# Banded attention in a fourteen-stage decoder kernel: the division is moved from the weights to the results, and the last chunk's order is rewritten

## The reference, cut to what matters

```python
_OFFSETS = list(range(41)) + [128, 96, 384]
idx = jnp.arange(T)[:, None] - deltas[None, :]
valid = idx >= 0
k_mod = k_g * (1.0 + scale_embed)
scores = jnp.einsum('bhtd,bhtjd->bhtj', q, k_mod) * scale
scores = scores + pos_bias.T[None, :, None, :]
scores = jnp.where(valid[None, None], scores, jnp.finfo(scores.dtype).min)
attn = jax.nn.softmax(scores, axis=-1)
out = jnp.einsum('bhtj,bhtjd->bhtd', attn, v_g)
out = out * if_gain[None, :, None, None]
out = out.transpose(0, 2, 1, 3).reshape(B, T, C)
return out @ w_out
```

## Time and profile before

| | |
|---|---|
| median of 3 runs | 3556.07 us (3554.3 to 3569.99) |
| profiled execution, its time | 3591.05 us |
| its span, mean granted TensorE clock | 3589.0 us, 0.94 |
| busy: TensorE matmuls, VectorE, ScalarE, GpSimd | 3165.8, 1804.1, 1185.1, 927.7 us |
| the stage: first product to last statistics | about 27 to 348 us |
| of it, chunks 1 to 3 and ending | 70 to 301 us, 301 to 348 us |

### The profile page before, as it was taken

The page is one execution under the profiler, slowest core; times in us unless marked ns, Lnnn a source line. Parts: engine busy times, 40 slices in busy tenths (PEclk is TensorE's granted clock), DMA queues, the critical chain, the costliest instruction groups (busy, mean ns, idle before and its releaser), DMA issues. The chain is left out here.

```text
span 3589.0 us, 74982 instructions
## 1 busy us (share of the span) xinstructions
PE 3165.8 (88%) x30324; PEld 2191.8 (61%) x30324; DVE 1804.1 (50%) x4518; ACT 1185.1 (33%) x2326; POOL 927.7 (26%) x771
## 2 busy tenths in 40 slices
PE   8886999999987878877777999779998899999989
PEld 3333555555666764655644555569997786566656
DVE  8887544543233463442386666543333663355543
ACT  1222323323223323221234556422222462144433
POOL 1000442442000000423426878611111210104001
PEclk9998999999989988988888999979999899999989
DMA  4223000000132020533601111068887200021100
GB/s 150 57 65 93 20 9 17 9 9 8 43 55 24 4 47 6 163 111 103 200 20 47 30 30 30 7 253 326 329 331 259 90 14 13 19 74 52 52 14 19
DMA packets 173982, 287.22 MB, mean 80 GB/s; under 512 B 79184, under 2 KB 144261, under 8 KB 164338
## 3 DMA queue, kind: packets, MB, share of 16 engines
q1 hardware_dynamic: 166194, 262.48, 23.5%
q0 software_dynamic: 7488, 20.46, 1.7%
HBM read 244.49 MB, written 28.48 MB: 76 GB/s over the span
## 5 line engine op out<-in xcount | busy, mean ns | idle before, releaser
L2646 PE MATMUL ps<-L_ffn_xsT,arena 128*128 128x128 f32 x2584 | 311.8, 280 | 20.2 <-DVE L_ffn_xsT L2445 16.1
L2646 PEld LDWEIGHTS ps<-L_ffn_xsT,arena 128*128 128x128 f32 x2584 | 303.6, 196 | 23.5 <-DVE L_ffn_xsT L2445 18.3
L161 POOL TENSOR_TENSOR rstd<-nsc,mhalf 112x4 f32<-112x4 f32 (+1 forms) x24 | 40.0, 1668 | 907.7 <-DVE nsc L154 906.7
L820 POOL TENSOR_TENSOR L_xattn_rn<-L_xattn_ss,mhalf 125x16 f32<-125x16 f32 (+1 forms) x64 | 185.6, 2901 | 258.6 <-DVE L_xattn_ss L883 258.6
L3329 POOL TENSOR_TENSOR L_xattn_pT<-L_xattn_pT,L_xattn_keep 125x678 int32<-125x678 int32 x128 | 190.2, 1507 | 71.5 <-ACT L_xattn_pT L3584 71.5
L2544 ACT ACTIVATE L_ffn_silu<-ps,arena 128x128 f32<-128x128 f32 x280 | 102.8, 367 | 269.0 <-PE ps L2646 253.7
L701 PE MATMUL ps<-L_attn_prod,arena 128*32 128x448 f32 (+28 forms) x672 | 158.9, 510 | 28.7 <-DVE L_attn_prod L510 28.4
L2454 DVE SCALAR_TENSOR_TENSOR L_ffn_hT<-ps,arena,L_ffn_silu 128x128 f32<-128x128 f32 x280 | 98.0, 351 | 155.5 <-ACT L_ffn_silu L2544 155.3
L2323 POOL DMA_INDIRECT L_ffn_rows_out<-L_ffn_ys,L_ffn_dest x78 | 79.5, 1020 | 339.6 <-DVE L_ffn_ys L2463 303.8
L997 PE MATMUL ps<-arena,L_xattn_cT 128*125 128x512 f32 x384 | 166.1, 592 | 0.0
L2659 PE MATMUL ps<-arena,L_ffn_hT 128*128 128x256 f32 x646 | 155.6, 385 | 0.1
(11 more groups left out here) (599 smaller groups left out, 6814.9 us busy)
## 6 DMA issues: line engine op xcount, KB each, us to landing
arena<-in_L_ffn_up SPq DMA_DIRECT2D x35, 2056.0 KB
arena<-in_L_ffn_down SPq DMA_DIRECT2D x35, 1152.0 KB
L_xattn_ctxT<-in_ctxT SPq DMA_DIRECT2D x48, 375.0 KB, 3.7
arena<-in_L_ffn_up SPq DMA_DIRECT2D x43, 384.0 KB
L_attn_a<-L_attn_skew SPq DMA_DIRECT2D x16, 784.0 KB, 5.1
L_xattn_ctx<-in_ctx SPq DMA_DIRECT2D x30, 375.0 KB
arena<-L_xattn_kp SPq DMA_DIRECT2D x64, 93.8 KB, 3.3
L_xattn_mask<-in_mask SPq DMA_DIRECT2D x32, 164.1 KB, 8.6
```

The source lines that it names most:

```text
L820: nc.gpsimd.tensor_tensor(rn[0:r, i], ss[0:r, i], core.mhalf[0:r, 0:H], ALU.pow).then_inc(po_r.step("root", i), 1)
L2646: ins = nc.tensor.matmul(ps[:, 2 + b % 4, half * TS:(half + 1) * TS], self.up(i % WU, k, half * HM + m), xsT[:, i % 2, k], start=(k == 0), ...
```

## The change

Exponentials go to memory undivided, as soon as ScalarE has made them. `divide` makes, instead of dividing, an operand `wide` of 112x256 values (in the memory of `xn`) that holds gain over denominator of each head, repeated 16 times. In `attend`, TensorE turns `wide` with two transposes ("spread") into the free half of bank 6, ahead of the 16 heads' matmuls, and a new VectorE step `scaled` multiplies `oT` with it, after ScalarE's copy. Projection and the next batch's attention wait for `scaled`. `wide` waits for the transposes of `xn`, and `xn` for the spread of the tail before.

The slots move: TURN from 29 to 26, ATTEND from 37 to 34, PROJECT from 39 to 38, UPDATE from 47 to 45; SCALED is at 36. In the ending all maxima and subtractions come ahead of all divisions, each batch's transposes ahead of its attention and the next batch's ones behind it, updates stand between the batches (before, all four stood last in VectorE's queue), and the context's normalisation is cut in three.

```diff
-        ve_n = [Progress(core, f"vector_norm{u}", ("den", 1), ("rden", 1), ("gain", 1), ("e", 1)) for u in range(U)]
+        ve_n = [Progress(core, f"vector_norm{u}", ("den", 1), ("rden", 1), ("wide", 1)) for u in range(U)]
+        ve_s, pe_s = [Progress(core, f"vector_scaled{u}", ("scaled", 1)) for u in range(U)], one("tensor", "spread", U)
...
-            TURN = {29 + 14 * (n // 4) + 2 * (n % 4): n for n in range(4 * U)}
-            ATTEND, PROJECT = ({n + 14 * u: u for u in range(U)} for n in (37, 39))
-            UPDATE = {min(47 + 14 * u, NI - 1): u for u in range(U)}
+            TURN = {26 + 14 * (n // 4) + 2 * (n % 4): n for n in range(4 * U)}
+            ATTEND, SCALED, PROJECT = ({n + 14 * u: u for u in range(U)} for n in (34, 36, 38))
+            UPDATE = {min(45 + 14 * u, NI - 1): u for u in range(U)}
...
-            MAX, SUB, EXP = ({n: 0, n + 2: 1, n + 6: 2, n + 12: 3} for n in (11, 12, 13))
-            DIVIDE = {16: 0, 20: 1, 26: 2, 28: 3}
-            TURN = {30 + 4 * n // 3: n for n in range(4 * U)}
-            ATTEND, PROJECT = ({n + 6 * u: u for u in range(U)} for n in (36, 37))
-            UPDATE = {80 + u: u for u in range(U)}
-            CONTEXT = 29
+            MAX, SUB, EXP = ({n + 2 * u: u for u in range(U)} for n in (11, 12, 13))
+            DIVIDE = {20 + u: u for u in range(U)}
+            TURN = {30 + 6 * (n // 4) + n % 4: n for n in range(4 * U)}
+            ATTEND, SCALED, PROJECT, UPDATE = ({n + 6 * u: u for u in range(U)} for n in (34, 35, 38, 40))
+            CONTEXT = {36: 0, 42: 1, 48: 2}
...
-                    sp.wait_ge(ve_n[u].sem, ve_n[u].at(c, "e"))
+                    sp.wait_ge(ac_e.sem, ac_e.at(c, "exp", u))
...
-                nc.vector.tensor_tensor(rden[:, u, :], rden[:, u, :], self.gain, ALU.mult).then_inc(ve.step("gain"), 1)
-                dve.wait_ge(ve.sem, ve.at(c, "gain"))
-                by_dist = e[c % 2][:, u].rearrange("p (j h) -> p j h", h=H)
-                nc.vector.tensor_tensor(by_dist, by_dist, rden[:, u, :].unsqueeze(1).to_broadcast([T, J, H]), ALU.mult).then_inc(ve.step("e"), 1)
+                if u == 0 and c + 2 < NCH:
+                    dve.wait_ge(pe_x.sem, pe_x.at(c + 2, "xT", KD - 1))
+                if c:
+                    dve.wait_ge(pe_s.sem, pe_s.at(c - 1, "spread", u))
+                nc.vector.tensor_tensor(wide[:, u].rearrange("p (h e) -> p h e", h=H), rden[:, u, :].unsqueeze(2).to_broadcast([T, H, HD]),
+                                        self.gain.unsqueeze(2).to_broadcast([T, H, HD]), ALU.mult).then_inc(ve.step("wide"), 1)
+
+            def scaled(c, u):
+                dve.wait_ge(pe_s.sem, pe_s.at(c, "spread", u))
+                dve.wait_ge(ac_o.sem, ac_o.at(c, "oT", u))
+                nc.vector.tensor_tensor(oT[:, u % 2], oT[:, u % 2], ps[:, 6, KD * T:2 * KD * T], ALU.mult).then_inc(ve_s[u].step("scaled"), 1)
...
                     if c + 1 < NCH and i == ahead.XN:
                         if c:
                             dve.wait_ge(pe_x.sem, pe_x.at(c, "xT", KD - 1))
+                        if c >= 2:
+                            dve.wait_ge(pe_s.sem, pe_s.at(c - 2, "spread", U - 1))
...
             def attend(c, u):
                 ten.wait_ge(ac_a.sem, ac_a.at(c, "aT", 4 * u + 3))
                 if u >= 1:
-                    ten.wait_ge(ac_o.sem, ac_o.at(c, "oT", u - 1))
+                    ten.wait_ge(ve_s[u - 1].sem, ve_s[u - 1].at(c, "scaled"))
                 else:
                     bank_free(c)
+                ten.wait_ge(ve_n[u].sem, ve_n[u].at(c, "wide"))
+                for b in range(KD):
+                    ins = nc.tensor.transpose(ps[:, 6, (KD + b) * T:(KD + b + 1) * T], wide[:, u, b * 128:(b + 1) * 128], core.ident[0:T, 0:T])
+                ins.then_inc(pe_s.step("spread", u), 1)
...
             def project(c, u):
-                ten.wait_ge(ac_o.sem, ac_o.at(c, "oT", u))
+                ten.wait_ge(ve_s[u].sem, ve_s[u].at(c, "scaled"))
```

More of the change, by code:

```diff
@@ L305, in build @@
         mx, den, rden = sb("mx", [T, U, H]), sb("den", [T, U, H]), sb("rden", [T, U, H])
+        wide = xn
         a, aT = sb("a", [T, 2, T * H]), sb("aT", [T, 2, H * T])
@@ L442, in front, with context_normed @@
                     normed(core, xn[:, u], U * c + u).then_inc(ve_x.step("xn", u), 1)
-            def context_normed():
+            def context_normed(part):
                 src = core.context
-                dve.wait_ge(ctx_in, 2 * DMA)
-                run.ahead_arrived(dve)
-                lnc.vector(dve, ve_c, 0, lambda t, q: src[:, t, :], lambda t: None)
-                dve.wait_ge(po_c.sem, po_c.at(0, "lncrs"))
-                for t in range(2 * ST):
+                if part == 0:
+                    dve.wait_ge(ctx_in, 2 * DMA)
+                    run.ahead_arrived(dve)
+                    lnc.vector(dve, ve_c, 0, lambda t, q: src[:, t, :], lambda t: None)
+                    return
+                if part == 1:
+                    dve.wait_ge(po_c.sem, po_c.at(0, "lncrs"))
+                for t in range(2 * ST if part == 1 else 0):
                     nc.vector.scalar_tensor_tensor(out=src[:, t, :], in0=src[:, t, :], scalar=lnc.mv[:, t, 0:1], in1=following.gain,
                                                    op0=ALU.subtract, op1=ALU.mult).then_inc(ve_c.step("gain", t), 1)
-                for t in range(2 * ST):
+                for t in range(2 * ST if part == 2 else 0):
                     dve.wait_ge(ve_c.sem, ve_c.at(0, "gain", t))
@@ L465, in biased @@
                         dve.wait_ge(written[u], (c - 1) * 2 * DMA)
+                        dve.wait_ge(ve_n[u].sem, ve_n[u].at(c - 2, "den"))
                 dve.wait_ge(pe_g.sem, pe_g.at(c, "turned", g))
@@ L524, in _ @@
                             divide(c - 1, after.DIVIDE[i])
+                        if i in after.SCALED:
+                            scaled(c - 1, after.SCALED[i])
                         if i in after.UPDATE:
@@ L527, in _ @@
                     if c == NCH:
-                        if i == after.CONTEXT:
-                            for u in range(U):
-                                dve.wait_ge(ve_w[u].sem, ve_w[u].at(0, "stats"))
-                            norm_vector(core, dve, lead, 0, U)
-                            context_normed()
+                        if i in after.CONTEXT:
+                            if after.CONTEXT[i] == 0:
+                                for u in range(U):
+                                    dve.wait_ge(ve_w[u].sem, ve_w[u].at(0, "stats"))
+                                norm_vector(core, dve, lead, 0, U)
+                            context_normed(after.CONTEXT[i])
                         continue
```

## The result

The changed kernel takes 3580.63 us (median of 20 runs, 3568.08 to 3589.84). Twenty runs of the kernel before, the three shown above among them, have a median of 3562.3 us (3553.15 to 3576.49). The ratio is 1.0047, 95% interval 1.0037 to 1.0057, so it is 0.47% or 16.7 us slower. The medians themselves differ by 18.3 us. The forecast was +10.2 us on a median of 3556.07: 3566 us, at most 3579. The measured time lies 14.6 us above the forecast and 1.6 above that bound.

A forecast was written before the change was run, and what follows sets the result against it. VectorE was taken to bound the chunks most of the time, TensorE where it turns weights, and one DMA queue to pace the ending. 3556 + 14.7 (chunks) - 4.5 (ending) = 3566 us; range -7 to +23, 3549 to 3579.

The forecast's parts named there:

- The mechanism: Chunks 1 to 3: VectorE idles 1.4 to 3 us before each SCALED; the last update's 4.15 us wait shrinks under 1.
- (b): Rival for chunks 1 to 3: TensorE keeps up, SCALED costs little, about 0; 3551 us; chance 0.20 together with (d).
- (d): Rival: only the ending changes, chunks within 2 us, same time as (b); chance 0.20 together with (b).
- (c): Rival: faster, 13.4 us of exponential waits vanish and SCALED finds its copy done; -23, 3533 us; chance 0.04.
- start of product 29 in the chunk: VectorE's first product after batch 1's division starts +0.2 us: a later exponential eats what two shorter divisions gave.
- waits of the four SCALED: VectorE's waits for attention and copy, batches 0 to 3 at full clock: 2.55, 1.95, 1.4 and 2.85 us.
- first SCALED of chunks 1 and 3: Batch 0's wait: 5.5 us in chunk 1 with TensorE's clock fallen; 2.55 up to 5 in chunk 3.
- the sum for the chunks: Chunks 1 to 3 lengthen by +5.6, +5.6 and +3.5 us, together +14.7.
- Rival (a), the clock: TensorE's clock falls in most batches, 3 us each; three further falls make +19, five +25 (3581 us); chance 0.14.
- The exponential: ScalarE's queue: exponentials move behind a copy of turned weights; batch 1's ends about 0.8 us later.
- The projection: TensorE's projection waits for SCALED, then for products not made; chunk end, last batch included, 15.9 us against 16.2, taken -0.1.
- The ending: After chunk 3: first write 4.3 us earlier, reads 6.2 to 6.6 apart; -4.5 us, bounds -5.5 to -2.

The follow-up runs named there:

- e1: Changed kernel with SCALED, projection and update at later slots in chunks 1 to 3, same work; chunks 227.7 us against 249.6, ratio to before 0.9989.
- e8: Kernel before in the changed kernel's slots, with a bare VectorE wait for ScalarE's copy and none of the new work; chunks 252.9 us, ratio 1.0044.
- e3: Kernel before in the chunks, with the changed kernel's ending; chunks 231.2 us, ending 42.1 us, ratio to before 1.0005.
- e5: Changed kernel's work in the slots of the kernel before, SCALED two slots behind attention; chunks 247.5 us, ratio to before 1.0039.
- e10: Changed kernel with only the projection moved, to SCALED's own slot ahead of the two held products; chunks 243.5 us, ratio to before 1.0029.
- e11: Changed kernel with later transposes, attention and first two divisions, SCALED seven slots after attention (four in last batch); chunks 209.1 us, ratio to before 0.9942.
- e6: e1 with transposes and attention two slots later, so ScalarE takes exponentials ahead of turned weights; chunks 224.2 us, ratio to before 0.9981.
- e9: Kernel before with a bare VectorE wait two slots after attention, projection two slots behind it (one in last batch), updates one later; chunks 248.9 us, ratio 1.0060.

## Why the prediction went as it did

**The mechanism was right.** VectorE stands before each of the 12 SCALED for ScalarE's copy, 1.7 to 3.8 us, and the 4.15 us at the last update became 0.87. e1 and e8 show it from both sides: the same work with other slots loses nothing, and the slots with the wait alone lose all (21.7 us). Rivals (b) and (d), no cost in the chunks, and (c), faster, are out. The terms against their measurements, chunk 2 where nothing else is said:

| term | predicted | measured |
|---|---|---|
| division | 1.95 | 1.98 |
| SCALED on the queue | 0.30 | 0.31 |
| spread, ahead of attention | 0.25 | 0.34 |
| SCALED after start of spread | 1.72 | 1.87 |
| start of product 29 in the chunk | +0.2 | +0.6 |
| waits of the four SCALED | 2.55, 1.95, 1.4, 2.85 | 3.79, 2.01, 1.73, 3.17 |
| first SCALED of chunks 1 and 3 | 5.5; 2.55 up to 5 | 3.78; 2.36 |
| chunks 1, 2, 3 | +5.6, +5.6, +3.5 | +5.8, +8.4, +4.1 |
| ending | -4.5 | -4.9 |

Start of product 29 is 180.77 - 150.23 = 30.54 us into the chunk before and 187.50 - 156.37 = 31.13 now.

**Two terms of the sum were too small: the base, 3556.07 us from three runs where twenty gave 3562.3 (6.2 us), and the sum for the chunks**, +14.7 against +18.3 (3.6 us), of which 2.8 lie in chunk 2. The step that failed there is the line that prices chunk 2 at +5.6 with its first SCALED at 2.55 us, at full clock. Its parts: the first SCALED there was priced at full clock, and the clock was at 0.81; it waited 3.79 where the same one in chunk 3, at 1.00, waited 2.36, 1.4 us of difference. The forecast had put one whole fall of 3 us into chunk 1 and none into chunk 2; ahead of the first SCALED there was one of 1.4 us in each. Part of this is luck: e3 ran the chunks of before again, and its chunk 2 had a fall and took 78.4 us, so measured against e3 the change costs 7.2 us in chunk 1, 7.1 in chunk 2 and 4.1 in chunk 3. The exponential of batch 1 came later than the 0.8 us that I took: VectorE's wait grew from 2.43 to 4.24, of which its own earlier arrival is 0.6, so 1.2 (+0.4). The waits of batches 2 and 3 were 0.3 each too short. In chunk 1 the parts missed in both directions (SCALED 3.78 instead of 5.5, the exponentials more) and only their sum was right.

**Rival (a), the clock**, is there in a small dose: three partial falls in after, one in each chunk, two of them ahead of a SCALED. It is not what makes the kernel slow: the granted clock was 0.98 in all three chunks against 0.96, 1.00 and 0.93 before, and chunk 2 of e5 had a clock of 1.00 and took 83.3 us, that of e10 82.05. I had weighed a rule of the Trainium skill, page "TensorE: Matmul & The Clock Gate", against this. Its Part 4, that transposes don't count as busy, would have the added transposes lower the clock; e11 has all of after's transposes (x450, x449 and x425 matmul records in both) and ran at 1.00 in all three chunks. No run here shows that transposes alone lower it. The page's section on HAM oscillation says that waits between bursts of matmuls bring the clock down. The traces agree in direction: the falls of after follow TensorE's 2.42, 2.48 and 2.41 us without products, and e11, where TensorE never stood longer than 1.55 us in the chunks, has no fall. But in e10 the same 2.48 us had none behind them. When a hole costs the clock stays open.

**The exponential.** The forecast had the queue place right (behind a copy of turned weights); e6 prices it at 3.5 us in the chunks, net of what SCALED waits more there.

**The projection** was taken to wait for SCALED and then for the products that are not made, and its late release was priced only for the last batch. e9 and e10 price it over all of them: 10.4 us for the two slots between wait and projection where no multiplication is in between (with updates one slot later), 6.1 where one is. The forecast's waits for SCALED contain its effect, but it doesn't name it as a cost of its own.

**The ending** went by its steps, counted from its start: first write 5.6 us predicted and 5.86 measured, last read 27.5 and 28.05, last attention 37.4 and 37.12, end 41.6 and 41.25. e3 has 42.1 in the ending with the chunks untouched. The first write stands 4.0 us earlier, since it no longer waits for the division, and the reads' distance is about as before (6.46 against 6.37), which accounts for most of the 4.9; what the new order of the steps gives by itself no run shows.

**What of the time was not the change.** The forecast of 3566 was put on a median of three runs, 3556.07, and twenty gave 3562.3: 6.2 us of the 14.6 by which it was short; that was chance of the three runs, and larger than any error of mechanism. As a difference it was +10.2 against +16.7 by the ratio, inside the bounds of -7 to +23. Of these 6.5 us, 3.6 are the chunks, -0.4 the ending, and 3.3 lie outside the stage; the difference of the medians, 18.3, is another 1.6 above the ratio's. The 3.3 stay open: over the thirteen kernels the change in whole time lies between 5.2 us below the change in the stage (e8: +21.0 in the stage and +15.8 in the time) and 6.1 above it (e11: -27.0 and -20.9), so a few microseconds of whole time don't belong to any step here.

## What to carry to other kernels

Where two engines feed each other through a short ring, a step that joins their queues must stand behind so much of the waiting engine's own work that the answer is there when it comes: here seven products instead of two between attention and multiplication (four in the last batch) turned +18 us into -3.5 in three chunks with the same instructions (projection and update moved along). Look at what lies behind each wait in the other queue as well: work that doesn't need the held products goes ahead of them, and a result that everyone waits for (the exponential) goes ahead of a copy that nobody does. When a change loses, time its slots and waits without its work; that shows whether the work or the place was wrong. Here it was the place: in other slots the same work took the chunks from 231.2 us to 209.1. How much of these 22 us needs the new work is not shown, since the old work was never run in e11's slots; of VectorE's busy time in the three chunks the new work takes off 3.4 us (198.8 before, 195.3 in e11).

## What the runs showed of the hardware

- The granted clock of the chunks did not follow the number of transposes: 0.98 in after and 1.00 in all three chunks of e11 at the same number of matmul records. It fell 37 times in chunks 1 to 3 of the fourteen kernels, each time while TensorE stood for 1.6 to 3.1 us without products or within 1.7 us after; 34 other such stops had no fall behind them, and e11, whose longest stop was 1.55 us, had none at all.
- A fall ahead of the first SCALED of a chunk cost about 1.4 us: that SCALED waited 3.78 and 3.79 us in after and 3.73 and 3.89 in e10 with a fall, and 2.36 and 2.35 without.
- Two fp32 transposes of 112x128 took 0.34 us from their start to the next matmul's, where eight in a row took 0.99, 0.12 each. The mean of the long row was too low a price for the pair; why is not shown.
- A 128x224 product of which one operand lies in PSUM took 0.39 us, and a 112x256 product of two broadcast operands 0.43: neither the broadcast nor PSUM cost what the strided 112x672 subtraction (1.34 us, 0.51 for 256 elements) might have led one to expect.
